# Four graph layers over 400000 sorted edges: 1400 chunks of edges counted densely where it was 1350, the last 50 with six rows of nodes

## The chip, the cores and the metric

The kernel runs on one core of one Trainium2 chip. The metric is the device time of one execution in microseconds, the median of three runs. One execution was profiled. The trace names the engines PE (TensorE; PEld are its weight loads), DVE (VectorE), ACT (ScalarE), POOL (GpSimd) and SP (SyncE).

## The reference

There are N = 12500 nodes with F = 64 features and E = 400000 edges, sorted by destination; sources are uniform, destinations lie as `12500 * u**2`, so low nodes have many edges and high ones few.

```python
x = _layernorm(x + _L0(edge_index, edge_type, x, ...))      # by source, with the relation: sigmoid(score) * x[dst], summed
x = _layernorm(x + _L1(x, src, dst, W, b))                  # h = segment_sum(x[src], dst), or x where there is no edge; h @ W.T + b
x = _layernorm(x + _L2(x, edge_index, edge_weight))         # segment_sum(x[src] * w, dst)
x = _layernorm(x + _L3(x, edge_index, edge_weight, edge_weight_n2))   # segment_sum(x[src] * (w2 * w), dst)
```

The first line sums over the source of each edge, the other three over its destination. These three are called the gather layers here, l = 0, 1 and 2 in the code; the first of them has no weights.

## The kernel before, in words

The edges are cut into C = 3125 chunks of 128, five chunks to a group (GC = 5). A gather layer sums a chunk in one of two ways.

**Dense**, for the first CD = 1350 chunks, whose destinations are so close that a chunk spans at most 3 to 5 nodes. For each chunk ScalarE makes the one-hot code of the source modulo 128 (`codes`, L921 to L932, times the weight in l = 1 and 2), and VectorE a one-hot tile of (source / 128, row) with rows x 98 columns by comparing a row of numbers with the chunk's key (`block_hots`, L1634). TensorE multiplies the two (`block_sums`, L1106); one to five chunks of a group form a block and are summed in one PSUM bank. VectorE adds each block into a window of 94 nodes (WC) in SBUF at a register offset (`block_add`, L1648). `PARTS` lists the ranges of chunks with the blocks in a group and the rows: (0, 200, (5,), 4) down to (1050, 1350, five blocks of one chunk, 5 rows), 1050 blocks in all. When a window is full (there are 28, two buffers), TensorE multiplies it with the features in 14 zones of seven matmuls (`flush_zone`, L1118), VectorE adds the result to the sums (`flush_add`, L1654), and ScalarE clears the zones (`clear`, L900).

**Tail**, for the remaining 1775 chunks, 355 steps of five (NT = 355). GpSimd gathers the 128 source rows of each chunk by an indirect DMA (L779) into a ring of R = 6 step buffers; VectorE makes the one-hot tile of the destinations (`tail_hots`, L1612) and in l = 1 and 2 weights it (`tail_weights`, L1621); TensorE sums the five chunks (L1139), and VectorE adds them (`tail_add`, L1663). Before the first gather of step n, GpSimd waits for TensorE's tail sum of step n - 6.

The order of both is written by a planner, `trailing_slots` (L121): it gives every block and every zone a cost, divides the sum by the number of steps less six, and puts blocks and zones into the steps of the tail as they come due (`BLOCK_END`, `ZONE_END`). In each step n TensorE does the block sums and zones that are due, then the tail sum of n. VectorE does the tail add of n - 1, the one-hot tiles of n + 2, the flush adds that are due, and for each block its add, followed by the tiles of later blocks for which there is room.

Room is given by rings. One-hot tiles and codes have BR = 10 chunks: a tile is made when the sum of the block ten chunks earlier is done. Block sums have PSD = 4 banks of PSUM (banks 0, 1, 2 and 6): the sum of block b waits for the add of block b - 4. Two banks (3, 4) hold tail sums, bank 5 the flush, bank 7 the row of numbers (`iota_p`, 490 columns).

Ahead of the layers stands the counting stage for the first line of the reference. It scatters the tail chunks from C0 = 1100 on with 2025 indirect DMAs of GpSimd (L700), 405 steps, with dense blocks of the first 1100 chunks beside them. Step by step SP loads rows of x: for groups of five-row chunks five small loads, for the later groups one of 64 rows. The keys of the dense chunks (`dense_keys`) are prepared here by VectorE.

## Time and profile before

| | us |
|---|---|
| median of 3 runs | 12297.09 |
| lowest, highest | 12291.68, 12302.24 |
| the profiled execution | 12289.04 |
| its span, first to last instruction | 12287.3 |
| mean granted TensorE clock | 0.775 of full |
| PE busy | 8780.1 (71%), 51577 instructions |
| DVE busy | 7811.6 (64%), 18656 |
| ACT busy | 5489.2 (45%), 12443 |
| POOL busy | 8308.1 (68%), 7419 |
| DMA | 410.51 MB, queue of POOL 16.1% and of SP 4.2% of 16 engines |

The busy shares are means over stages: about 3930 us of counting, some 160 us that finish the first line, and three gather layers of 2625 to 2691 us with normalisations between them. An fp32 matmul stands in the trace as two records. Waits that the page puts down to "remote" have a release that it can't name.

### The profile page before, as it was taken

What the parts mean: (1) busy time and instruction counts of PE and PEld (TensorE: products, weight loads), DVE (VectorE), ACT (ScalarE), POOL (GpSimd) and SP (SyncE); (2) the same over time, 40 slices, a digit from 0 to 9 for tenths busy, and PEclk for the clock granted to TensorE, in tenths of its full rate; (3) what the DMA queues carried; (4) which work ended last, traced back from release to release, by engine and by line L of the source; (5) the groups of instructions that cost most, each with busy time, mean ns of one, the idle gap of its engine ahead of it and who ended that gap; (6) DMA issues with size and microseconds to landing.
All of it is one profiled execution on the core that took longest, in us unless ns stands there. A gap on an engine that the chain in (4) does not pass through costs nothing. (4 is left out here: it accounts for less than half of the span.)

```text
span 12287.3 us, 173107 instructions
## 1 busy us (share of the span) xinstructions
PE 8780.1 (71%) x51577; PEld 6089.0 (50%) x51578; DVE 7811.6 (64%) x18656; ACT 5489.2 (45%) x12443; POOL 8308.1 (68%) x7419
## 2 busy tenths in 40 slices
PE   4777777777775455556656787777787787777776
PEld 2555556565554334444445445444445445444444
DVE  8777776766664765555554776656555776665655
ACT  4655544444442443333222665444433655444333
POOL 5888788888888566666665566666665566666665
PEclk7776777677776566676777898888888898888887
DMA  5333333333334211111111111111111111111111
GB/s 142 44 41 37 37 37 39 38 39 38 39 38 65 57 24 24 24 24 24 24 23 25 28 25 25 25 25 25 24 23 27 28 24 25 25 25 25 24 23 29
DMA packets 673100, 410.51 MB, mean 33 GB/s; under 512 B 473202, under 2 KB 582516, under 8 KB 670913
## 3 DMA queue, kind: packets, MB, share of 16 engines
q0 software_dynamic: 465120, 260.68, 16.1%
q1 hardware_dynamic: 203244, 135.37, 4.2%
q8 instruction: 432, 7.08, 0.2%
q10 hardware_dynamic: 3814, 3.37, 0.1%
q14 instruction: 490, 4.01, 0.1%
HBM read 291.44 MB, written 107.44 MB: 32 GB/s over the span
## 5 line engine op out<-in xcount | busy, mean ns | idle before, releaser
L779 POOL DMA_INDIRECT mem<-xt,mem x5325 | 5038.0, 946 | 3010.2 <-issue 1397.3
L1106 PE MATMUL ps<-mem 128*128 128x392 f32 (+5 forms) x6750 | 3015.5, 556 | 1108.3 <-issue 426.1
L700 POOL DMA_INDIRECT table<-mem,idx x2025 | 3154.4, 1558 | 749.6 <-issue 596.4
L1648 DVE TENSOR_TENSOR mem<-mem,ps 128x392 f32 (+2 forms) x3150 | 1802.8, 572 | 2143.1 <-remote 1243.3
L921 ACT ACTIVATE mem<-iota_f,mem 128x128 f32<-128x128 f32 x4050 | 1272.1, 390 | 2657.8 <-remote 1307.0
L1634 DVE TENSOR_SCALAR mem<-ps,mem 128x392 f32<-128x392 f32 (+5 forms) x4050 | 2456.5, 626 | 0.0
L1118 PE MATMUL ps<-mem,xs 128*64 128x94 f32 (+1 forms) x16464 | 2036.2, 279 | 473.9 <-issue 457.6
L1118 PEld LDWEIGHTS ps<-mem,xs 128*64 128x64 f32 (+1 forms) x16464 | 1758.5, 161 | 1129.8 <-issue 1091.2
L1106 PEld LDWEIGHTS ps<-mem 128*128 128x128 f32 (+1 forms) x6750 | 1156.1, 192 | 2019.8 <-issue 1452.7
L900 ACT COPY mem<-zero_c 128x658 f32<-128x658 f32 x1176 | 836.0, 732 | 1791.6 <-remote 1364.0
L1139 PE MATMUL ps<-mem 128*64 128x64 f32 (+1 forms) x10650 | 1120.8, 248 | 697.4 <-issue 675.9
L1139 PEld LDWEIGHTS ps<-mem 128*64 128x64 f32 (+1 forms) x10650 | 936.8, 159 | 1121.9 <-issue 1097.2
L984 PE MATMUL ps<-mem 128*128 128x392 bf16 (+2 forms) x2200 | 730.6, 471 | 585.5 <-DVE mem L1409 485.5
L1007 PE MATMUL ps<-mem 128*128 128x128 f32 x5684 | 866.4, 308 | 290.8 <-ACT mem L826 276.4
L1007 PEld LDWEIGHTS ps<-mem 128*128 128x128 f32 x5684 | 797.6, 219 | 344.6 <-ACT mem L826 320.1
L1424 DVE TENSOR_TENSOR acc<-acc,ps 128x512 f32<-128x512 f32 (+1 forms) x700 | 472.8, 677 | 745.2 <-PE ps L1007 660.5
L1663 DVE TENSOR_TENSOR acc<-acc,ps 64x64 f32 (+1 forms) x1065 | 223.0, 209 | 1044.9 <-remote 772.8
L1409 DVE TENSOR_TENSOR mem<-mem,ps 128x784 f32 (+2 forms) x800 | 787.8, 985 | 153.1 <-issue 67.0
L932 ACT ACTIVATE mem<-mem 128x128 f32<-128x128 f32 x2700 | 848.4, 390 | 17.7
L1035 PE MATMUL ps<-mem 64*128 64x64 f32 (+1 forms) x4050 | 719.5, 338 | 74.6 <-ACT mem L839 74.6
L1035 PEld LDWEIGHTS ps<-mem 64*128 64x128 f32 (+1 forms) x4050 | 655.2, 246 | 210.5 <-issue 102.4
L854 ACT COPY mem<-ps 128x320 f32<-128x320 f32 x405 | 171.8, 424 | 1250.5 <-DMA table<-mem,idx 832.2
(173 smaller groups left out, 7516.3 us busy)
## 6 DMA issues: line engine op xcount, KB each, us to landing
mem<-xt,mem POOLq DMA_INDIRECT x5325
mem<-key_rows SPq DMA_DIRECT2D x405, 160.0 KB
table<-mem,idx POOLq DMA_INDIRECT x2025
table<-mem POOLq DMA_DIRECT2D x3, 6304.0 KB
mem<-table SPq DMA_DIRECT2D x42, 448.0 KB, 5.2
xt<-xs SPq DMA_DIRECT2D x9, 896.0 KB
mem<-in_x_dram SPq DMA_DIRECT2D x413, 16.0 KB
mem<-in_x_dram SPq DMA_DIRECT2D x250, 1.2 KB
```

The costliest lines, as they stand in the source:

```text
L700: pool.indirect_dma_start(out=tables[i % NTAB][:, :], out_offset=bass.IndirectOffsetOnAxis(ap=idx[:, i % (IDXS * GC):i % (IDXS * GC) + 1], ...
L779: pool.indirect_dma_start(out=gbuf[:, o:o + F], out_offset=None, in_=xt[l][:, :], in_offset=bass.IndirectOffsetOnAxis(ap=src_q[q % 2].bitc ...
L900: act.copy(dense[zi // FZ % 2][:, lo * WC:hi * WC], zero_c[:, :].to_broadcast([P, (hi - lo) * WC])).then_inc(cleared[l], 1)
L921: ins = act.activation(lo_d[:, k * P:(k + 1) * P], iota_f[:, 0:P], ACT.Abs, bias=nslo_q[q % 2][:, c + k:c + k + 1])
L932: ins = act.mul(lo_l[:, o + k * P:o + (k + 1) * P], lo_d[:, k * P:(k + 1) * P], wd_q[q % 2][:, c + k:c + k + 1])
L1007: last = pe.matmul(ps_s[u % 2][:, k * P:(k + 1) * P], at_sb[u % 2][:, k * P:(k + 1) * P], xb[s_ % 2], start=True, stop=True)
L1035: last = pe.matmul(ps_m[:, k * F:(k + 1) * F], bts[0:kw, k * P:(k + 1) * P], rhs, start=True, stop=True)
L1106: last = pe.matmul(ps_d[b % PSD][:, 0:w], lo_l[:, r * P:(r + 1) * P], blk_l[:, r * DT:r * DT + w], start=(k == 0), stop=(k == parts - 1))
L1118: last = pe.matmul(ps_f[0:M, :], xs[:, t * XW:t * XW + M], dense[s_ % 2][:, t * WC:(t + 1) * WC], start=(t == 0), stop=(t == T - 1), skip_ ...
L1139: last = pe.matmul(ps_w[n % 2][0:M, :], gbuf[:, o:o + M], ohr[:, q:q + WD], start=(k == 0), stop=(k == GC - 1), skip_group_check=True)
L1634: ins = v.tensor_scalar(blk_l[:, r * DT:r * DT + w], iota_p[:, 0:w], kd_q[q % 2][:, at + k:at + k + 1], None, ALU.is_equal)
L1648: v.tensor_tensor(at, at, new, ALU.add).then_inc(d_add[l], 1)
```

## The change

CD goes from 1350 to 1400, so a layer has 345 steps of the tail and 1100 blocks. Chunks 1350 to 1399 are a new part with six rows each (D = 6), and since 6 x 98 = 588 columns are more than a bank of 512, each of these blocks is made in two halves of 294 columns: two one-hot comparisons, the second against a copy of the key less 294 (`kd_half`), two matmuls with the same weights into the two banks of a pair (`ps_d2`, banks 0 and 1 or 2 and 3), and one add over both banks. So that the four banks pair up, the tail sums move to banks 4 and 5 and the flush to bank 6. The new blocks take turns with two pairs: the sum of b waits for the add of b - 2, and the first of them for all adds before it. Their tiles use a ring of BX = 8 (`hot_after`). Windows stay 94 wide, but the largest offset in one is 88 and not 89; that gives 30 windows and not 28. With more blocks, more windows and fewer steps, the planner's cost of a step goes from 5.93 to 6.49. In the counting stage groups 270 to 279 now count as dense ones for SP's loads and for the keys.

```diff
-CD = 1350
+C6 = 1350
+CD = 1400
-D = 5
-DT = D * T
+D = 6
+DT = 5 * T
+DX = D * T
+BX = 8
-         (700, 1050, (1, 1, 1, 1, 1), 4), (1050, CD, (1, 1, 1, 1, 1), D)]
+         (700, 1050, (1, 1, 1, 1, 1), 4), (1050, C6, (1, 1, 1, 1, 1), 5),
+         (C6, CD, (1, 1, 1, 1, 1), D)]
+def hot_after(b):
+
+    c = BLOCKS[b][0] + BLOCKS[b][1] - 1
+    if c >= C6:
+        return BLOCK_OF[max(c - BX, C6 - 1)]
+    return BLOCK_OF[c - BR] if c >= BR else -1
-SEGS0, SEG_OF0 = segments(NB0, WD, 6)
+SEGS0, SEG_OF0 = segments(NB0, WD, 5)
-            if not is_block and z % FZ == 0 and zones[-1] < z:
+            if not is_block and z % FZ == 0 and (zones[-1] < z or blocks[-1] < SEGS[z // FZ + 1]):
+        kd_half = sb("kd_half", [P, CD - C6])
-        ps_d = [ps[:, k * BK:k * BK + DT] for k in (0, 1, 2, 6)]
-        ps_w = [ps[:, (3 + p) * BK:(3 + p) * BK + WD] for p in range(2)]
-        ps_f = ps[:, 5 * BK:5 * BK + WC]
+        ps_d = [ps[:, k * BK:k * BK + DT] for k in range(PSD)]
+        ps_d2 = [ps[:, 2 * p * BK:2 * (p + 1) * BK].rearrange("p (h c) -> p h c", h=2)[:, :, 0:DX // 2] for p in range(2)]
+        ps_w = [ps[:, (4 + p) * BK:(4 + p) * BK + WD] for p in range(2)]
+        ps_f = ps[:, 6 * BK:6 * BK + WC]
...
                     pe.wait_ge(blk_done[l], b + 1)
+                    if c >= C6:
+                        pe.wait_ge(d_add[l], b if c == C6 else b - 1)
+                        for h in range(2):
+                            at = (c - C6) % BX * DX + h * DX // 2
+                            last = pe.matmul(ps_d2[b % 2][:, h, :], lo_l[:, c % BR * P:(c % BR + 1) * P],
+                                             blk_l[:, at:at + DX // 2], start=True, stop=True)
+                        last.then_inc(blk_sum[l], 1)
+                        return
...
+                    link(v.tensor_scalar(kd_half[:, :], kd[:, C6:CD], -float(DX // 2), None, ALU.add))
...
                 def block_hots(b, l=l, blk_l=blk_l):
                     c, parts = BLOCKS[b]
-                    if c + parts > BR:
-                        v.wait_ge(blk_sum[l], BLOCK_OF[c + parts - 1 - BR] + 1)
+                    if hot_after(b) >= 0:
+                        v.wait_ge(blk_sum[l], hot_after(b) + 1)
...
+                    if c >= C6:
+                        r = (c - C6) % BX * DX
+                        v.tensor_scalar(blk_l[:, r:r + DX // 2], iota_p[:, 0:DX // 2], kd_q[q % 2][:, at:at + 1], None,
+                                        ALU.is_equal)
+                        v.tensor_scalar(blk_l[:, r + DX // 2:r + DX], iota_p[:, 0:DX // 2], kd_half[:, c - C6:c - C6 + 1],
+                                        None, ALU.is_equal).then_inc(blk_done[l], 1)
+                        return
...
-                    new = ps_d[b % PSD][:, 0:rows * T].rearrange("p (s d) -> p s d", s=T)
+                    if rows == D:
+                        at = dense_h[s_ % 2][:, :, :, at]
+                        new = ps_d2[b % 2].rearrange("p h (s d) -> p h s d", d=rows)
+                    else:
+                        at = dense_s[s_ % 2][:, :, at]
+                        new = ps_d[b % PSD][:, 0:rows * T].rearrange("p (s d) -> p s d", s=T)
                     v.tensor_tensor(at, at, new, ALU.add).then_inc(d_add[l], 1)
```

## Rows read from the trace of the kernel before

**Rows 1.** Busy time by stage: PE, PEld, DVE, ACT, POOL, granted clock, DMA, GB/s

```profile
1500.00:2500.00 1000.00, 759.28 (x4647) 587.07 (x4647) 697.57 (x2087) 494.15 (x934) 827.65 (x534) 0.73 0.38 38
4088.00:6713.00 2625.00, 1526.82 (x10369) 1177.54 (x10370) 1473.80 (x3136) 884.26 (x2000) 1673.63 (x1774) 0.69 0.11 24
6801.00:9487.00 2686.00, 2127.87 (x11718) 1304.88 (x11718) 1653.23 (x3488) 1302.84 (x3344) 1680.32 (x1774) 0.86 0.11 24
9541.00:12232.00 2691.00, 2116.90 (x11718) 1298.23 (x11718) 1654.71 (x3489) 1303.83 (x3345) 1680.91 (x1774) 0.87 0.11 24
```

**Rows 2.** Groups of instructions: count, busy us, mean ns, idle before and its releasers

```profile
L779 POOL DMA_INDIRECT mem<-xt,mem x5325 | 5038.0, 946 | 3010.2 <-issue 1397.3 <-remote 1026.7 <-PE ps L1139 542.5
L700 POOL DMA_INDIRECT table<-mem,idx x2025 | 3154.4, 1558 | 749.6 <-issue 596.4 <-ACT mem L854 123.5 <-DMA table<-mem,idx 27.3
L1612 DVE TENSOR_TENSOR mem<-ps,mem 128x320 f32<-128x320 f32 x1065 | 508.5, 478 | 0.8 <-issue 0.7
L1663 DVE TENSOR_TENSOR acc<-acc,ps 64x64 f32 (+1 forms) x1065 | 223.0, 209 | 1044.9 <-remote 772.8 <-PE ps L1139 208.8 <-issue 62.2
```

**Rows 3.** Gathers (L779) in 200 us: busy (count), clock; layers one and two

```profile
4088.00:4300.00 212.00, 139.06 (x148) 0.57 0.11 24
...
4700.00:4900.00 200.00, 126.34 (x135) 0.67 0.11 25
6850.00:7050.00 200.00, 111.94 (x118) 0.92 0.10 21
7450.00:7650.00 200.00, 124.64 (x132) 0.85 0.11 26
8850.00:9050.00 200.00, 127.75 (x135) 0.84 0.11 24
```

**Rows 4.** Block adds (L1648) in 200 us of layer two: 294 columns, then 490

```profile
7450.00:7650.00 200.00, 53.25 (x117) 0.85 0.11 26
8850.00:9050.00 200.00, 49.49 (x75) 0.84 0.11 24
```

**Rows 5.** One-hot tiles of dense chunks (L1634) in 200 us of layer two

```profile
6850.00:7050.00 200.00, 114.78 (x208) 0.92 0.10 21
7450.00:7650.00 200.00, 60.21 (x117) 0.85 0.11 26
8850.00:9050.00 200.00, 54.14 (x75) 0.84 0.11 24
```

**Rows 6.** Waits in layer two, 7000 to 9400 us: total, times, longest

```profile
POOL mem L779 <- remote: 314.4, 176, 2.7
POOL mem L779 <- PE ps L1139: 158.0, 74, 4.4
```

**Rows 7.** Order of time in layer two: start, us, instruction, idle before and releaser

```profile
7613.11 0.80 PE L1139 MATMUL ps<-mem 128*64 128x64 f32 x10
7617.70 0.94 POOL L779 DMA_INDIRECT mem<-xt,mem  x1 [0.30 <-issue]
7620.16 0.22 DVE L1663 TENSOR_TENSOR acc<-acc,ps 64x64 f32 x1 [1.95 <-remote]
7620.20 0.94 POOL L779 DMA_INDIRECT mem<-xt,mem  x1 [1.56 <-remote]
```

**Rows 8.** Tail adds (L1663) in two stretches at the end of layer two

```profile
9449.10:9467.10 18.00, 0.21 (x1) 0.72 0.09 19
9482.30:9491.80 9.50, 1.27 (x6) 0.55 0.08 17
```

**Rows 9.** Flush matmuls (L1118), 200 us of layer two: PE, PEld

```profile
8850.00:9050.00 200.00, 54.78 (x481) 46.87 (x481) 0.84 0.11 24
```

**Rows 10.** Block matmuls (L1106), 200 us: 294 columns, then 490

```profile
7450.00:7650.00 200.00, 92.39 (x236) 43.32 (x236) 0.85 0.11 26
8850.00:9050.00 200.00, 88.65 (x148) 27.14 (x147) 0.84 0.11 24
```

**Rows 11.** Order of time on POOL in the counting stage, the step with the keys

```profile
618.25 1.54 POOL L700 DMA_INDIRECT table<-mem,idx  x1 [5.51 <-DMA table<-mem,idx]
```

More of the change, by code:

```diff
@@ L335, in program @@
         rows1 = rows0 + 2 * ND0 + NTT
-        sbase, sbase0 = arena[0:1, rows1:rows1 + NSEG], arena[0:1, rows1 + 64:rows1 + 64 + NS0]
+        sbase, sbase0 = arena[0:1, rows1:rows1 + NSEG], arena[0:1, rows1 + 32:rows1 + 32 + NS0]
         nq_row = stat[0:1, 0:Q]
+        assert NSEG <= 32 and NS0 <= 32 and rows1 + 32 + NS0 <= 8455
         STAGED = AR + 2 * CQ * P + 2 * NTAB * BN
@@ L363, in program @@
         ps_s = [ps[:, (5 + p) * BK:(6 + p) * BK] for p in range(2)]
-        ps_d = [ps[:, k * BK:k * BK + DT] for k in (0, 1, 2, 6)]
-        ps_w = [ps[:, (3 + p) * BK:(3 + p) * BK + WD] for p in range(2)]
-        ps_f = ps[:, 5 * BK:5 * BK + WC]
-        ps_x = ps[:, 5 * BK + 2 * P:5 * BK + 3 * P]
+        ps_d = [ps[:, k * BK:k * BK + DT] for k in range(PSD)]
+        ps_d2 = [ps[:, 2 * p * BK:2 * (p + 1) * BK].rearrange("p (h c) -> p h c", h=2)[:, :, 0:DX // 2] for p in range(2)]
+        ps_w = [ps[:, (4 + p) * BK:(4 + p) * BK + WD] for p in range(2)]
+        ps_f = ps[:, 6 * BK:6 * BK + WC]
+        ps_x = ps[:, 6 * BK + 2 * P:6 * BK + 3 * P]
         iota_p = ps[:, 7 * BK:7 * BK + DT]
@@ L1552, in _ @@
             dense_s = [d.rearrange("p (s d) -> p s d", s=T) for d in dense]
+            dense_h = [d.rearrange("p (h s d) -> p h s d", h=2, s=T // 2) for d in dense]
             offs = Row(v, "dve_o", offs_i, WC - D)
@@ L1642, in block_add @@
                     rows = ROWS_OF[b]
-                    at = dense_s[s_ % 2][:, :, ds(offs.value(b), rows)]
+                    at = ds(offs.value(b), rows)
                     if b:
@@ L1665, in hots_up_to @@
                 def hots_up_to(b, added):
-                    while b < NBLK and (BLOCKS[b][0] + BLOCKS[b][1] <= BR or
-                                        BLOCK_OF[BLOCKS[b][0] + BLOCKS[b][1] - 1 - BR] < added):
+                    while b < NBLK and hot_after(b) < added:
                         block_hots(b)
```

## The prediction

> **What bounds the kernel now.** I read the busy time by stage first, then the pace of the gathers in stretches of 200 us, then the waits of GpSimd, and last the order of time around one step. The stages [rows 1]: the counting stage (a slice of it is shown) keeps GpSimd at 827.65 of 1000 us with 534 scatters, 1.87 us each, of which 1.558 us is the instruction itself [rows 2]; it is GpSimd's. Then come the three gather layers, 2625, 2686 and 2691 us, two thirds of the span. In none of them is an engine full: GpSimd is busy for 62 to 64%, VectorE for 56 to 62%, TensorE for 58% in the first and 79% in the others. What the reader should see is the next view: in the body of the layers 132 to 135 gathers are issued in 200 us [rows 3], one step of five gathers in 7.4 to 7.6 us. That holds in the first layer with bf16 blocks and in the second with fp32, at a granted clock of 0.67 and 0.84, and with 117 block adds in 200 us as with 75 [rows 4]. Only the opening of layers two and three is slower: 118 gathers in 200 us [rows 3], while VectorE makes 208 one-hot tiles there [rows 5], 0.96 us for a dense chunk.
>
> GpSimd alone could do a step in 5 x (0.946 + 0.30) = 6.2 us. It waits for TensorE's tail sums to free a gather buffer, 314.4 us in 176 waits whose event isn't shown plus 158.0 us in 74 that are put down to TensorE's line, in 2400 us of layer two [rows 6]. The order of time shows how [rows 7]: TensorE's tail sum is recorded at 7613.11, VectorE takes its result only at 7620.16, and GpSimd, which has issued the last gather of a step at 7617.70, goes on at 7620.20. So TensorE's results reach the other engines late and at about the time at which the last gather of a step has landed. By the Trainium skill (Perfetto Trace Analysis, Summary: the profiler window per engine type) the end of a TensorE instruction in a profile is an estimate, and the time until its semaphore is seen lies outside of it; that is the reading taken here, and no row tells which part of these 6 us it is. When there are no gathers left to issue, six tail adds come within 9.5 us, and while seven flush zones are due by the plan there is one add in 18 us [rows 8]. I read this as a pace of about 7.45 us that is tied to the cycle of the gathers as long as a step's dense work fits into it.
>
> **The change, part by part.** I sum against the profiled execution, 12289.04 us (span 12287.3 and 1.7 around it); the median of the runs is 8.05 us higher, and the sum is carried over to it.
>
> 1. Ten steps (of 355) go from each layer: 50 gathers of 0.946 us, 50 tail matmuls, ten tail adds of 0.209 us and ten one-hot tiles of 0.478 us [rows 2], with their weighting in two layers. At the mean pace of each layer, 2625/355 = 7.39, 7.57 and 7.58 us, that is 10 x 22.54 = **-225 us**. If the pace isn't the gathers', this term is only the work of the steps: on VectorE 0.69 us and the weighting, for which I estimate as much as for the tile: some -12 us a layer.
>
> 2. The planner puts the same early blocks into fewer steps: the first 30 steps of a layer hold 275 chunks and not 255 (worked out from the cost formula in the code). In layers two and three that opening goes by the chunk, 0.96 us each [rows 5]: 20 x 0.96 x 2 = **+38 us**. In layer one the opening is no slower than the body (148 gathers in its first 212 us [rows 3]), and I take nothing. The bound below is zero, the bound above 58 us (all three).
>
> 3. In the body the blocks come denser, 3.27 in a step and not 3.04. The trace has such a contrast: with 117 adds in 200 us there are 132 gathers, with 75 there are 135 [rows 3, 4]. That is 4.4 blocks in a step of 7.58 us against 2.8 in one of 7.41, 0.1 us for a block. 0.23 x 0.1 x 315 steps is 7 us a layer; with a step's work also made of more flush zones (1.33 and not 1.21) I take 12, **+36 us**. Below is zero; above, if each added flush zone is paid in full: 28 zones in a layer (two more windows of 14), each 1.59 us on TensorE (54.78 us for 481 records, 14 to a zone [rows 9]), 45 us a layer, 134 us in all.
>
> 4. The 50 new blocks of a layer. Each chunk is now two matmuls of 294 columns into two banks. A 294-column block takes 0.78 us on TensorE (92.39 us, 118 blocks), a 490-column one 1.20 us (88.65 us, 74 blocks) [rows 10], so two are 1.57 us: +0.37 over a block of five rows. VectorE makes two tiles of 294, 0.515 us each (60.21/117), where one of 490 takes 0.722 (54.14/75) [rows 5]: +0.31. Its add over 588 columns has no row; between 455 ns at 294 and 660 ns at 490 [rows 4] the slope is 1.05 ns a column, which gives an estimate of 0.76 us, +0.10. ScalarE's codes for 50 chunks lie beside it and are hidden by an engine that is idle more than half of the body. The new wait is on the sums: block b needs the add of b-2, where it was b-4, because two pairs of banks replace four. Behind this wait on TensorE are the flush zones and the tail sum of the step, and for the tail sum wait VectorE's next tail add and GpSimd's buffer. With 50 blocks in some 20 steps, 2.5 in each, this is where the pace may break. The bound below is zero; above, everything in series, 0.78 us for a block, 39 us a layer, and without limit by rows if the late arrival of [rows 7] is paid per pair. I take half of it, 20 us a layer, since the nearest rows (layer one's opening [rows 3], with blocks of five chunks and a ring with room for two) keep their pace: **+60 us**.
>
> 5. The switch from four banks to two pairs: the first new block waits for all adds, and the first eight new tiles for the last old sum. One drain of the chain, a block sum and an add and the way between, 3 to 7 us by [rows 7]; I take 5, **+15 us** for three.
>
> 6. The moved banks (tail sums, flush, fix-up) and the window of block offsets (88 and not 89 rows) cost nothing: the same instructions. On the destination indices of the inputs, cut into chunks of 128, no edge lies outside of its five or six rows or of its window, with the old bounds or the new, so the branches for stray edges stay empty.
>
> 7. The counting stage: groups 270 to 279 load ten times five small rows where it was one, on SP's queue; and the keys of the dense chunks are prepared in one run more, with the halved copy: eight linked VectorE instructions in one step. GpSimd's pace of 1.87 us covers the loads; in the step that holds this work GpSimd once waited 5.51 us [rows 11]. Eight more of these instructions at an estimated 0.5 us (a small one of this kind, the tile of 320 elements, takes 0.478 [rows 2]) are **+4 us** if paid in full, zero if not.
>
> Sum: -225 + 38 + 36 + 60 + 15 + 4 = **-72 us**: 12217 for the profiled execution, 12225 for the median.
>
> On TensorE's clock the rows show 0.69 granted in layer one, where the engine is busy for 58% of the time, and 0.86 and 0.87 in the others, at 79% [rows 1]: shares of the upper level, 2.4 GHz, in a mix with 1.2. The Trainium skill (TensorE: Matmul & The Clock Gate, What's actually happening) has it that activity releases the throttle; by that rule denser work would be paid back in part by the clock, and the trace agrees in direction. The sum by it would lose TensorE's share of item 4, 9 us a layer, and be near -99 us.
>
> **The rivals.** (a) The pace holds whatever is put into a step: only items 1, 2 and 7 count, -183 us, 12114. For it: 135 gathers with TensorE busy for 58% in one layer and 79% in the other. Against: the 132 at the densest stretch.
>
> (b) The two pairs of banks set the new stretch: if a pair of blocks needs one cycle of 7.4 us, 50 blocks take 186 us where 20 steps take 150; that is 36 us a layer more, in place of the 20 of item 4. With item 3 halfway to its upper bound (67 and not 36) it ends at 12225 + 48 + 31 = 12304: no change that can be told. For it: the adds follow the sums late. Against: room for two was enough in the opening of layer one.
>
> (c) Slower: TensorE, with the late arrival of its results, is the true bound, and the even pace is the planner's, which gives every step the same cost. Place: the body of all three layers. Price: the work added to it, 50 x 1.57 + 28 x 1.59 = 123 us a layer, less ten tail sums of about 1 us, 113 us a layer, 339 in all: 12636. It decides from the point at which a step's work no longer fits between two steps of gathers; if only half of it shows, 12467. For it: GpSimd waits in most steps, the steps at the end that hold only flush zones take as long as the others, 7 zones took 18 us [rows 8], and the planned cost of a step rises by 9% (5.93 to 6.49). Against: layer one, with 58% on TensorE, is only 2.3% shorter than layer two with 79%.
>
> (d) The change doesn't do what it says: a longer detour, like stray edges. By the indices there are none; 0.02. It would end above 12470.
>
> **How the numbers follow.** Forecast 0.48, (a) 0.12, (b) 0.15, (c) 0.23, (d) 0.02. The predicted time is the forecast's, 12225. The range takes in (a), (b) and the lower half of (c): 12105 to 12470, with about 0.04 below and 0.14 above. The forecast's own range is 12150 to 12270. A measurement tells about 0.2%, 25 us, from no change: faster 0.60 (the forecast and (a)), same 0.15, slower 0.25.
>
> **What would show it.** Right: 135 gathers in 200 us of the body as before, layers near 2590, 2665 and 2670 us, 1725 gathers in each. Item 2: the opening still at 0.96 us for a chunk. Item 4: in the last tenth of a layer, with adds of 588 columns at 0.76 us, gathers slow to no less than 125 in 200 us. Rival (b): under 115 there, with waits of TensorE's block sums for the block adds above the present ones. Rival (c): 125 or fewer gathers in 200 us in all of the body, and TensorE's busy share over 85% in layers two and three. I am wrong altogether if the counting stage moves by more than 15 us.

## The result and the profile after

The changed kernel takes 12106.87 us (median of 4 runs, 12100.94 to 12110.4), the kernel before beside it 12297.33: a ratio of 0.9847, interval 0.9835 to 0.9859. That is 190 us less where the forecast had 72, and within 8 us of rival (a), 12114. It lies 2 us above the lower end of the stated range, 12105, and outside of the forecast's own range of 12150 to 12270. The profiled execution has a span of 12108.7 us. Of all executions below one, of CD = 1450, took 12257.48 us at a granted clock of 0.586, where its three others took 10698 to 10705 us at 0.83 to 0.84; it is left out of the ratios.

Busy time by stage, for the stages of [rows 1] (PE, PEld, DVE, ACT, POOL, granted clock, DMA, GB/s):

```profile
1500.00:2500.00 1000.00, 758.58 (x4663) 586.23 (x4662) 696.21 (x2087) 495.99 (x938) 831.96 (x537) 0.73 0.38 38
4083.00:6649.00 2566.00, 1526.63 (x10769) 1193.09 (x10769) 1547.72 (x3268) 922.63 (x2088) 1626.69 (x1725) 0.71 0.11 24
6741.00:9369.00 2628.00, 2143.62 (x12210) 1321.20 (x12210) 1721.18 (x3611) 1358.49 (x3480) 1632.86 (x1724) 0.90 0.11 24
9425.00:12053.00 2628.00, 2132.14 (x12211) 1309.47 (x12212) 1721.93 (x3612) 1360.63 (x3480) 1632.54 (x1724) 0.91 0.11 24
```

The layers are shorter by 59, 58 and 62 us (first to last gather 2625.8, 2687.1 and 2691.5 us before; 2566.6, 2629.5 and 2629.2 after), each with ten steps fewer; they begin 5 us earlier. A mean step went from 7.40, 7.57 and 7.58 to 7.44, 7.62 and 7.62 us. TensorE and VectorE do more in less time, and the granted clock rose in every layer.

The pace is the old one all along. Gathers (now L796) in stretches of layers one and two, busy time of POOL with the count, clock, as in [rows 3]; then the block adds (L1687) in four of these stretches, as in [rows 4]:

```profile
4083.00:4295.00 212.00, 137.88 (x146) 0.60 0.11 24
4695.00:4895.00 200.00, 126.32 (x134) 0.69 0.11 24
6790.00:6990.00 200.00, 113.43 (x120) 0.96 0.10 22
7390.00:7590.00 200.00, 125.49 (x133) 0.89 0.11 25
8390.00:8590.00 200.00, 127.24 (x134) 0.86 0.11 25
9190.00:9340.00 150.00, 94.84 (x100) 0.93 0.10 23
```

```profile
4695.00:4895.00 200.00, 58.00 (x128) 0.69 0.11 24
7390.00:7590.00 200.00, 55.69 (x122) 0.89 0.11 25
8390.00:8590.00 200.00, 52.17 (x79) 0.86 0.11 25
9190.00:9340.00 150.00, 31.27 (x41) 0.93 0.10 23
```

The last stretch holds most of the 50 six-row blocks, and its 100 gathers in 150 us are 7.5 us a step: the pace of the rest. What the new blocks cost their engines is in the groups of equal shape (line, engine, operation, tiles, count, busy us, mean ns, idle before and its releasers):

```profile
L1122 PE MATMUL ps<-mem 128*128 128x294 f32 x400 | 135.9, 462 | 54.7 <-DVE mem L1687 43.3 <-issue 8.5 <-DVE mem L1663 1.6
L1687 DVE TENSOR_TENSOR mem<-mem,ps 128x588 f32 x150 | 114.1, 761 | 62.8 <-remote 34.1 <-PE ps L1122 15.1 <-issue 12.5
```

The add over 588 columns takes 761 ns, as estimated. TensorE's 400 records are the fp32 blocks of layers two and three; before them it was idle for 54.7 us, and 43.3 us of these are put down to VectorE's adds, the wait on b-2. The waits of layer two, 6940 to 9320 us (line waited for: us, times, longest), show that GpSimd waits about as it did in [rows 6]:

```profile
POOL mem L796 <- remote: 294.2, 173, 2.8
POOL mem L796 <- PE ps L1164: 198.1, 89, 5.7
PE ps L1131 <- DVE mem L1687: 100.9, 73, 5.7
PE ps L1122 <- DVE mem L1687: 20.8, 13, 6.6
```

So the gain is the ten steps, and almost nothing was paid for what they were exchanged for. The experiments ask three things: what sets the pace, what the dense work costs at it, and what the pace itself is made of.

### The profile page after: what moved, and what is told of

The parts are those of the page before. It is cut to its first block and busy times, and to the rows that moved or that the text cites. A ratio compares the mean times of both kernels' runs of the same rounds, so it can differ in the third digit from the quotient of the medians.

```text
span 12108.7 us, 177157 instructions
## 1 busy us (share of the span) xinstructions
PE 8810.7 (73%) x52953; PEld 6130.1 (51%) x52954; DVE 8021.3 (66%) x19055; ACT 5642.3 (47%) x12807; POOL 8169.7 (67%) x7269
## 3 DMA queue, kind: packets, MB, share of 16 engines
q8 instruction: 443, 7.26, 0.2%
## 5 line engine op out<-in xcount | busy, mean ns | idle before, releaser
L796 POOL DMA_INDIRECT mem<-xt,mem x5175 | 4895.3, 946 | 2973.9 <-issue 1331.8
L1131 PE MATMUL ps<-mem 128*128 128x392 f32 (+5 forms) x6750 | 2932.4, 540 | 1066.2 <-DVE mem L1687 425.9
L1687 DVE TENSOR_TENSOR mem<-mem,ps 128x392 f32 (+3 forms) x3300 | 1919.9, 582 | 1866.7 <-remote 990.2
L938 ACT ACTIVATE mem<-iota_f,mem 128x128 f32<-128x128 f32 x4200 | 1319.2, 390 | 2694.7 <-remote 1307.7
L1143 PEld LDWEIGHTS ps<-mem,xs 128*64 128x64 f32 (+1 forms) x17640 | 1807.7, 156 | 1033.7 <-issue 985.9
L917 ACT COPY mem<-zero_c 128x658 f32<-128x658 f32 x1260 | 896.5, 732 | 1430.1 <-remote 960.0
L1164 PE MATMUL ps<-mem 128*64 128x64 f32 (+1 forms) x10350 | 1043.4, 246 | 525.1 <-issue 505.4
L1164 PEld LDWEIGHTS ps<-mem 128*64 128x64 f32 (+1 forms) x10350 | 886.7, 158 | 949.7 <-issue 925.6
L1052 PE MATMUL ps<-mem 64*128 64x64 f32 (+2 forms) x4050 | 719.0, 338 | 74.7 <-ACT mem L856 64.6
L1052 PEld LDWEIGHTS ps<-mem 64*128 64x128 f32 (+2 forms) x4050 | 654.7, 245 | 210.9 <-issue 114.0
```

The source lines that it names most:

```text
L796: pool.indirect_dma_start(out=gbuf[:, o:o + F], out_offset=None, in_=xt[l][:, :], in_offset=bass.IndirectOffsetOnAxis(ap=src_q[q % 2].bitc ...
L917: act.copy(dense[zi // FZ % 2][:, lo * WC:hi * WC], zero_c[:, :].to_broadcast([P, (hi - lo) * WC])).then_inc(cleared[l], 1)
L938: ins = act.activation(lo_d[:, k * P:(k + 1) * P], iota_f[:, 0:P], ACT.Abs, bias=nslo_q[q % 2][:, c + k:c + k + 1])
L1052: last = pe.matmul(ps_m[:, k * F:(k + 1) * F], bts[0:kw, k * P:(k + 1) * P], rhs, start=True, stop=True)
L1131: last = pe.matmul(ps_d[b % PSD][:, 0:w], lo_l[:, r * P:(r + 1) * P], blk_l[:, r * DT:r * DT + w], start=(k == 0), stop=(k == parts - 1))
L1143: last = pe.matmul(ps_f[0:M, :], xs[:, t * XW:t * XW + M], dense[s_ % 2][:, t * WC:(t + 1) * WC], start=(t == 0), stop=(t == T - 1), skip_ ...
```

## The experiments

They were run in six groups, each beside the kernel before on the same chip. **There are two paces, by group**: the kernel before took 12289.99, 12202.6, 12292.42 and 12201.62 us in four groups (the slower pace, that of the result above), 10941.28 and 10942.37 in two. Times are compared within a group; where a time is held against one of another group, the text says so. The two groups at the faster pace ran on two chips, those at the slower one on three others, one of them met twice (12289.99 and 12202.6 us). That it is the chip that decides is likely by this and not shown. Of a code edit the first or the main lines are printed. Kernels that leave work out, and those with the smaller ring or with fewer waits on the changed kernel, were executed once. A "step" below is the time from the first to the last gather of a layer over its number of steps, for layers one, two and three.

### What sets the pace

**One gather of five in a step** (the tail sum uses its rows five times):

```diff
-                    for k in range(GC):
+                    for k in range(1):
                         o = (n % R) * GW + k * XW
```

> The changed kernel with one gather in a step where it has five; the four others are left out, and all five tail matmuls read the chunk that is there. All work of the other engines stays. Theory G (the cycle of a step's five gathers sets the pace of 7.4 to 7.6 us): the step falls to what the other engines need, about 4.5 us in layer one and 6 to 6.5 in the others, which takes 350 us or more off each layer; below 11100 us. Theory W (TensorE's dense work sets the pace, and the even pace is the planner's): 12107 us within 60. Theory V (VectorE's chain of adds and tiles sets it): the same as W.

9952.7 us beside 12289.99; steps of 4.81, 5.80 and 5.79 us. Stage 7000 to 9000 us of it, columns as above:

```profile
7000.00:9000.00 2000.00, 1872.39 (x11976) 1186.88 (x11975) 1707.62 (x3583) 1335.48 (x3427) 327.23 (x339) 0.98 0.05 11
```

With four of five gathers gone TensorE is busy for 94% at a clock of 0.98, and 5.8 us is what it needs for a step of the changed kernel in layers two and three; in layer one VectorE (busy for 92%) needs 4.8. Theory G is met: what the changed kernel takes beyond that, up to 7.44 and 7.62 us, belongs to the gathers. By itself this doesn't rule out rival (c), in which TensorE with its late results is the bound, since the late results may go with the gathers. The next run asks for that.

**The dense work made lighter**, with five gathers: one matmul of seven in each flush zone; block adds over one row only; a ring of four step buffers and not six.

```diff
-                    for t in range(*ZONES[z]):
+                    for t in (ZONES[z][0] if z < FZ - 1 else T - 1,):
```

> The changed kernel with one matmul in a flush zone where it has seven; the six others are left out, so TensorE loses six sevenths of 2079 us of flush matmuls, some 590 us a layer, 1.7 us of a step. Waits, adds and clears stay. Theory G: within 60 us of 12107. Theory W: the layers lose most of these 1.7 us a step, 400 to 590 us each; 10400 to 10900. Theory V: as G.

11918.91 us; steps of 7.26, 7.43 and 7.41. With some 1.7 us of TensorE's work gone from a step, and its busy share from 7000 to 9000 us down from 82 to 70%, the step loses 0.2 us of 7.6. The kernel ends about 180 us below the changed one, three times the 60 us of theory G and far from the 1200 to 1700 us of theory W: the dense work isn't quite free, and it isn't the bound, so rival (c) at its price is out. The granted clock fell with the work, from 0.90 to 0.82 in that stretch.

```diff
-                        at = dense_h[s_ % 2][:, :, :, at]
+                        at = dense_h[s_ % 2][:, :, :, at][:, :, :, 0:1]
```

> The changed kernel with block adds over one row of the block where it has three to six; the other rows are left out. VectorE's 3300 adds take about 0.2 us where they took 0.58, some 1.2 us a step. Theory G and theory W: within 60 us of 12107, if the later buffers come free a little earlier perhaps 50 us less. Theory V: 1.2 us off 1035 steps, about 10900.

12091.19 us, steps of 7.43, 7.57 and 7.62: VectorE's adds cost next to nothing, some 10 us of the kernel.

```diff
-R = 6
+R = 4
```

> The changed kernel with a ring of four step buffers for the gathers where it has six; the result is the same. In the kernel before, the tail add of a step comes 38 to 40 us after its gathers. If this lag is a fixed delay on the way (theory L), the step becomes 39/4 = 9.8 us and the kernel some 2000 us slower. If some engine has a fixed rate and the lag is only the queue ahead of it (G, W and V alike), the ring doesn't matter: within 60 us of 12107.

12083.25 us, steps of 7.43, 7.59 and 7.59. The tail add now trails the last gather of its step by 24 to 25 us and not by 39 to 40, so the ring is always full, whatever its size, and its size isn't what limits.

### What the parts of the change cost

**Six-row blocks alone**: chunks 1300 to 1349 get them, CD stays 1350, so 355 steps as before. At both paces:

```diff
-C6 = 1350
-CD = 1400
+C6 = 1300
+CD = 1350
```

> The changed kernel with C6 = 1300 and CD = 1350: 355 steps and 28 windows as before the change, but the last 50 dense chunks have six rows, two banks and a pair's turns. Its difference to the kernel before is the price of the blocks of six rows by themselves (items 4 and 5 of the prediction). Theory G (the gathers' cycle sets the pace, a step's dense work fits into it): 12297 us within 15. The prediction's items 4 and 5: some 0.41 us on VectorE and 0.37 on TensorE for each of 150 blocks in part, and three drains: 12297 + 75 = 12372.

> C6 = 1300 and CD = 1350 again, for the price of the six-row blocks at the other pace. With the kernel before at 12297 and steps of 7.4 to 7.6 us: theory G 12297 within 20; the prediction's items 4 and 5: 12372. With the kernel before at 10941: 10948 again, and nothing new.

At the faster pace 10947.59 us, a ratio of 1.0007 (0.9997 to 1.0016); at the slower one 12225.23 us, 1.0018 (1.0008 to 1.0028), beside 12202.6: 23 us (10 to 34) for items 4 and 5, where the prediction had 75 and theory G at most 20. The two profiles show what the paces are. Gathers of the stretch 7000 to 9000 us (busy POOL, count, clock), first at the faster, then at the slower pace, and GpSimd's waits at the faster one from 7000 to 8500 us:

```profile
7000.00:9000.00 2000.00, 1472.98 (x1553) 0.95 0.15 30
```

```profile
7000.00:9000.00 2000.00, 1273.70 (x1342) 0.87 0.13 25
```

```profile
POOL mem L796 <- issue: 364.8, 1197, 0.3
```

At the faster pace a step is 6.24 to 6.27 us, GpSimd's own 5 x (0.946 + 0.30), and it waits for nobody; the tail add trails the gathers by 3 us.

**The exchange rate**: the kernel before with 50 dense chunks fewer, the changed one with 50 and with 100 more (for these two the list of windows needs more room, so the source of zeros is half as wide).

```diff
-CD = 1350
+CD = 1300
```

> The kernel before with CD = 1300: 365 steps, 1000 blocks, 26 windows, planned cost of a step 5.44. Theory G: ten steps more in a layer at 7.4 to 7.55 us, 12297 + 3 x 74.5 = 12520, less 10 to 20 for a lighter opening. Theory W (dense work sets the pace): 50 blocks of five rows and 28 zones less, 1.2 and 1.59 us each, 105 us a layer: 12297 - 315 + 30 = 12010.

```diff
-CD = 1400
+CD = 1450
-zeros = arena[:, 8455:8455 + ROWS * F // P // 16]
+zeros = arena[:, 8849:8849 + ROWS * F // P // 32]
```

> The changed kernel with CD = 1450: 335 steps, 1150 blocks, 32 windows, planned cost of a step 7.08. (The source of the zeros for the tables is half as wide and read twice as often, so that the longer rows of indices have room; a few us at the start.) Theory G with the need of TensorE as the other bound, which the run with one gather puts at 5.8 us of a step: 5.8 x 7.08/6.49 = 6.3 us, still under 7.6, so another ten steps are saved: 12107 - 180 = 11927, within 40. Prediction's sum, with its give-backs: 12107 - 72 = 12035.

> The changed kernel with CD = 1500: 325 steps, 1200 blocks, 34 windows, planned cost of a step 7.71. TensorE's need by the same scaling is 5.8 x 7.71/6.49 = 6.9 us, near the 7.6 of the gathers' cycle. Theory G: 11927 - 170 = 11757, within 60; the pace in layers two and three would begin to give way, to 7.8 us. If the need of TensorE adds to the gathers' (theory A, each gather takes 0.45 us from TensorE, 7.6 = 5.8 + 4 x 0.45), a step is 6.9 + 1.8 = 8.7 us in layers two and three and the kernel is at 12250 or more, slower than with 1400.

All at the faster pace, against 10941.28 us: CD = 1300 11138.43, 1.0179 (1.0162 to 1.0196), that is +197 us for 30 steps more, 6.6 each (the expectation's two times were for the slower pace); CD = 1450 10703.94, 0.978 (0.9761 to 0.98); CD = 1500 10740.38, 0.9817 (0.9801 to 0.9833). Steps: 6.24, 6.27, 6.27; then 6.24, 6.43, 6.43; then 6.27, 6.77, 6.76. Here the mechanism of rival (c) sets in: from CD = 1450 on TensorE's need passes GpSimd's 6.24 us, and the ten steps less of 1500 lose more than they bring. The need could be forecast: 5.8 us scaled by the planned cost of a step gave 6.3 and 6.9 us, and layers two and three took 6.43 and 6.77. Stretch 7000 to 9000 us of CD = 1500:

```profile
7000.00:9000.00 2000.00, 1873.38 (x11751) 1187.15 (x11750) 1681.85 (x3401) 1287.99 (x3283) 1378.90 (x1440) 0.97 0.14 28
```

TensorE is at 94%, its level with a single gather in a step, and GpSimd issues 1440 gathers where it could 1600.

**The change and CD = 1450 at the slower pace**:

> The changed kernel itself. In the last group of runs the kernel before took 10941 us and not 12297, with a step of 6.24 us, which is GpSimd's five gathers and their gaps with nothing else, and without the stalls inside of TensorE's groups. If that is met again: theory G gives ten steps of 6.25 us in each of three layers, 10941 - 188 = 10755, within 15, since TensorE's 5.8 us fit into 6.24. With the other pace (kernel before at 12297): 12107 again.

> CD = 1450 again. With the kernel before at 12297: theory G (the larger of the gathers' cycle, 1.49 us for each of five, and TensorE's need of 6.3 us) 11930 within 40; theory A (each gather beyond the first takes 0.45 us from TensorE, on top of its need) 6.3 + 1.8 = 8.1 us in layers two and three, about 12250. With the kernel before at 10941: 10704 again.

The change: 12020.56 us, 0.9855 (0.9838 to 0.9871), the result once more. CD = 1450: 11875.14 us, 0.9736 (0.972 to 0.9752), steps of 7.41, 7.57 and 7.59. There is still room in a step at this pace: twenty steps less bring 327 us, ten bring 182. CD = 1450 beats the kernel before at either pace, and the changed one at the slower; at the faster pace the changed one wasn't run, and CD = 1500 wasn't at the slower.

### What the pace is made of

**Three gathers and four in a step** (as in the first experiment, with 3 and 4 for 1):

> The changed kernel with three gathers in a step where it has five; two are left out, and the tail matmuls of the last three chunks read the third. Theory G (a step is the larger of 1.49 us for each gather, 4.5 us, and the need of the other engines, which the run with one gather shows as 4.8 us in layer one and 5.8 in the others): about 9960 us, as with one gather. Theory A (each gather beyond the first takes 0.45 to 0.6 us from TensorE): 4.8 + 1.2 = 6.0 and 5.8 + 0.9 = 6.7 us, about 10900. If the kernel before is met at 10941, no stalls are there and theory A has nothing to act on: about 9960 by both.

> The changed kernel with four of the five gathers in each step (TensorE's fifth product takes the fourth chunk's rows; results are not the reference's). Theory C: a step takes 4 x 1.49 = 5.96 us in layer one and the larger of 5.96 and TensorE's 5.8 in the others, with few stalls of TensorE there: 10150 to 10250 in all. A rival F, in which the late answers set in only when the gathers are close to one another and cost a fixed 1.2 us a step over GpSimd's own 1.25 us a gather: 5.0 + 1.2 = 6.2 us in all layers, 10350 to 10450.

10050.8 us beside 12202.6 and 10803.25 us beside 12292.42. Theory A's 10900 for three gathers is out; theory G's 9960 is 91 us too low. Steps: 5.05, 5.82, 5.83 with three; 6.10, 6.40, 6.39 with four. In layer one, where the rest needs 4.8, that is GpSimd's 1.25 us for each gather and 1.3, 1.1 and 1.2 us on top (three, four, five gathers): a fixed part once in a step, rival F. By 1.49 us a gather three would have left layer one at its 4.8, and it took 5.05; of four gathers F had 6.2 and theory C 5.96, and 6.10 lies between them. In layers two and three it is 1.4, 0.2 more than F had. (The totals expected of four gathers were added up some 300 us too low; the steps are the test.) TensorE's groups of matmuls show stalls in their middle, where it waits for no semaphore. I count the pairs of neighbouring weight loads of one line that start over 0.6 us apart with no wait between them: 8 in layer two with one gather in a step, 14 with three, 104 with four, 350 with five (337 us from start to start; 287 pairs when the kernel was run again beside that with three gathers); none before the layers, and 22 at the faster pace. Some of these are no stalls, for at a granted clock of 0.50 a block's matmul alone comes near 0.6 us or over it. With the granted clock above 0.95 between the two loads the counts are 0, 3, 61 and 195 with one, three, four and five gathers, and 0 at the faster pace.

**Half the rows; a quarter of each row**, with as many gathers:

```diff
-                            out=gbuf[:, o:o + F], out_offset=None, in_=xt[l][:, :],
+                            out=gbuf[0:h, o:o + F], out_offset=None, in_=xt[l][:, :],
```

(h is 64 rows from the seventh step of the first layer on; the second kernel takes 16 numbers of a row in place of 64, and has no other edit.)

> The changed kernel with each gather taking 64 rows instead of 128 from the seventh step of the first layer on, so half the rows and half the bytes with as many gathers (the other half of each buffer keeps old data; results are not the reference's). Theory C, the cycle belongs to the count of gathers: a step stays at 7.4 to 7.6 us in all layers where the kernel before has 7.4 to 7.6, and the kernel within 60 us of the changed one. Rival L, the cycle is made by the landing of rows (descriptors or bytes): a step falls to GpSimd's own 6.2 us or to the 5.8 that TensorE needs, and the kernel to 10750 or less. If the kernel before runs at 6.24 us a step here, a fall below 6.24 shows only that GpSimd's instruction got shorter.

> The changed kernel with each gather taking rows of 16 numbers (64 bytes) instead of 64 (256 bytes) from the seventh step of the first layer on: as many gathers and rows, a quarter of the bytes, from the first quarter of the table (results are not the reference's). Theory C, count of gathers: a step stays at 7.4 to 7.6 us. Rival L in its form for bytes: 6.2 us or less, the kernel near 10750. Rival L in its form for descriptors: this one stays at 7.4 to 7.6 and the one with half the rows falls.

12104.79 and 12093.08 us beside 12292.42; steps of 7.44, 7.64, 7.60 and 7.43, 7.59, 7.60, and 331 and 322 stalls. Neither the rows nor the bytes that land matter: it is the number of gathers that counts, and rival L is out in both forms. GpSimd's groups in the two profiles:

```profile
L797 POOL DMA_INDIRECT mem<-xt,mem x5175 | 4689.3, 906 | 3178.4 <-issue 1318.2
```

```profile
L797 POOL DMA_INDIRECT mem<-xt,mem x5175 | 4892.4, 945 | 2957.4 <-issue 1325.2
```

With half the rows each instruction is 40 ns shorter, 0.2 us a step, and the step isn't: GpSimd waits longer instead. That the instruction took 945 ns with a quarter of the bytes, where it took 946, agrees with the Trainium skill (Perfetto Trace Analysis, DMA Instruction — SWDGE (GPSIMD)), by which its profiled end is when the descriptors have been written, not when the data have moved.

**Fewer waits**: GpSimd waits once for two or three free buffers and issues ten or fifteen gathers in a row.

```diff
-                    if n >= R:
-                        pool.wait_ge(agg_done[l], n - R + 1)
+                    if n >= R and n % 3 == 0:
+                        pool.wait_ge(agg_done[l], n - R + 3)
```

> The changed kernel in which GpSimd waits for a free buffer only before every second step of gathers, for two buffers at once (tail sum n - 4 and not n - 6), so ten gathers follow one another. Runs so far give a step as 1.25 us for each gather plus 1.1 to 1.4 us once a step (five gathers 7.44 and 7.62, four 6.10 and 6.39, three 5.05). Theory D: the fixed part is one pause of GpSimd for each wait, since TensorE's signals come through only while no gathers are being issued; with one wait for two steps a step takes 6.25 + 0.6 to 0.7 = 6.9 us, all layers together 2380 us each and less, the kernel near 11430. Rival E: TensorE is slowed by the gathers in flight themselves and GpSimd waits for it, as often as it is; the step stays at 7.4 to 7.6 and the kernel at 12050 to 12150, or comes out longer because the ring is in effect one step shorter.

> The same with one wait for three buffers before every third step (tail sum n - 3), fifteen gathers in a row. Theory D: 6.25 + 0.4 to 0.5 = 6.7 us a step, the kernel near 11200, if what a step holds for TensorE then still fits. Rival E: as before, 12050 to 12200; a stall of TensorE that grows with the run of gathers would make it longer still.

> CD = 1450 as before (335 steps; 7.41, 7.57 and 7.59 us a step at the slower pace, 6.24 and 6.43 at the faster one), and GpSimd waits once before every third step for three buffers, fifteen gathers in a row. The two runs with fewer waits fell on a group in which GpSimd never waits (6.24 us a step), so they could tell nothing of theory D. If the kernel before runs at 12200 to 12300 here: D (the fixed part is one pause for each wait) gives 6.25 + 0.4 to 0.5 us a step, 6.7, the kernel near 11000; E (TensorE is slowed by the gathers in flight) gives 7.4 to 7.6 as before, the kernel within 60 us of 11870, or longer. If the kernel before runs at 10940, both give 10700 and nothing is told apart.

The first two met the faster pace: 10828.65 and 10829.86 us beside 10942.37, with steps of 6.25, 6.36, 6.35 and 6.24, 6.37, 6.36. From 7000 to 8500 us GpSimd waits for nobody there, so they tell nothing of the pause. The third met the slower pace, and it takes **14125.84 us** beside 12201.62, 1.1581 (1.1562 to 1.16), with steps of 8.98, 10.18 and 10.15 us. Theory D had 11000. Without two of three waits it takes 2250 us more than the same kernel with all of them (11875 in another group, beside a kernel before of 12202.6). The wait before step n is also for a later tail sum, that of step n - 4 where it was n - 6, as with a smaller ring (the expectations say n - 3). No run parts this from the fifteen gathers in a row; a ring of four cost nothing above. The order of time shows what happens. One train of fifteen gathers in layer two, start us, us, engine, line, operation, tiles, count, idle before and releaser:

```profile
8505.01 0.94 POOL L796 DMA_INDIRECT mem<-xt,mem  x1 [11.26 <-PE ps L1164]
8507.21 0.58 DVE L1687 TENSOR_TENSOR mem<-mem,ps 128x392 f32 x1
8508.24 0.58 DVE L1687 TENSOR_TENSOR mem<-mem,ps 128x392 f32 x1
8509.26 0.58 DVE L1687 TENSOR_TENSOR mem<-mem,ps 128x392 f32 x1
...
8509.79 0.66 PEld L1164 LDWEIGHTS ps<-mem 128*64 128x64 f32 x10 [0.56 <-issue]
...
8516.51 0.56 DVE L1687 TENSOR_TENSOR mem<-mem,ps 128x392 f32 x1
8519.31 0.56 DVE L1687 TENSOR_TENSOR mem<-mem,ps 128x392 f32 x1 [1.71 <-PE ps L1131]
8521.60 1.14 PEld L1164 LDWEIGHTS ps<-mem 128*64 128x64 f32 x10 [1.10 <-issue]
8522.71 0.95 POOL L796 DMA_INDIRECT mem<-xt,mem  x1 [0.30 <-issue]
8523.54 0.56 DVE L1687 TENSOR_TENSOR mem<-mem,ps 128x392 f32 x1 [3.13 <-remote]
8524.25 1.65 PE L1131 MATMUL ps<-mem 128*128 128x392 f32 x2 [1.32 <-DVE mem L1687]
8526.38 0.56 DVE L1687 TENSOR_TENSOR mem<-mem,ps 128x392 f32 x1 [1.74 <-PE ps L1131]
8527.40 0.55 DVE L1687 TENSOR_TENSOR mem<-mem,ps 128x392 f32 x1
8528.40 0.58 DVE L1687 TENSOR_TENSOR mem<-mem,ps 128x392 f32 x1
...
8531.85 0.66 PEld L1164 LDWEIGHTS ps<-mem 128*64 128x64 f32 x10 [0.56 <-issue]
8532.92 0.95 POOL L796 DMA_INDIRECT mem<-xt,mem  x1 [9.26 <-PE ps L1164]
```

At the start of the train, at 8507, VectorE gets TensorE's block sums one each microsecond; in its second half one in three; from 8526.4 on, 1.6 us after the last data landed (8524.82 by the landings in the trace), again one each microsecond. The ten weight loads of a tail sum take 0.66 us early in the train as after it, and 1.14 us at 8521.60; that is the clock, which is granted at 0.50 from 8521.5 to 8522.8 and at 1.00 in the two other places. The busy times (PE, PEld, DVE, ACT, POOL, clock):

```profile
8505.00:8509.00 4.00, 3.50 (x11) 1.50 (x9) 3.96 (x11) 2.65 (x8) 3.08 (x4) 1.00 0.09 16
8513.00:8517.00 4.00, 1.69 (x4) 0.47 (x4) 2.86 (x8) 1.39 (x5) 3.09 (x4) 1.00 0.19 34
8517.00:8521.00 4.00, 1.88 (x4) 0.80 (x4) 1.70 (x4) 2.50 (x7) 3.08 (x4) 0.79 0.13 25
8526.00:8530.00 4.00, 4.00 (x19) 2.78 (x20) 3.62 (x8) 3.65 (x11) 0.00 (x0) 0.56 0.00 0
8530.00:8534.00 4.00, 4.00 (x35) 2.70 (x33) 2.33 (x6) 1.60 (x3) 0.95 (x1) 1.00 0.00 0
```

Over the 88 whole trains of 7600 to 10300 us (18.5 us each, then 11.7 us of pause) I counted TensorE's semaphore updates for sums of any kind, its weight loads and VectorE's block adds. The last column takes each block sum that ends in the stretch by the trace, and gives the median time until VectorE's add of it starts:

| time | updates per us | weight loads per us | block adds per us | us from sum to add |
|---|---|---|---|---|
| first 2 us of the train | 0.78 | 6.8 | 0.47 | 1.9 |
| 2 to 4 | 0.56 | 5.2 | 0.56 | 1.4 |
| 4 to 10 | 0.27 | 5.6 | 0.39 | 7.9 |
| 10 to 18 | 0.13 | 1.2 | 0.10 | 10.9 |
| first 2 us after its end | 0.14 | 0.7 | 0.11 | 5.1 |
| third us after it | 3.45 | 2.7 | 0.44 | 3.7 |
| fourth | 1.41 | 3.4 | 0.70 | 2.0 |
| 9 to 11.6 us after | 1.0 | 6.4 | 0.66 | 0.8 |

The updates are not all recorded, 1035 of 1150 for the block sums of the layer, and between 4 and 10 us the recorded ones of block sums (0.15 per us) are fewer than the adds that each need one (0.39). So the first column is too low there; the adds and their sums are complete, 1150 each, and the last column rests on them. From 4 us into a train on, the trace shows TensorE loading weights at its rate, while its sums are taken up 8 to 11 us after their recorded end. Then it has little left to start on, and a burst of updates comes 2 to 3 us after the train's end, 2.0 per us for block sums of which TensorE ends 0.1 per us at that time. As TensorE's recorded ends are modelled, no row tells whether the sums themselves are late or only their signals. The clock adds to the cost: it is granted at 0.72 from 10 us on and at 0.51 in the 4 us after the train, and over layer two at 0.80, where the kernel with all waits had 0.94.

So of theory D's premise the better part is shown (most signals come through where no gathers are in flight) and its conclusion is wrong: the rest of the step lives on these signals, and the longer train starves it. Rival E, TensorE's side slowed by gathers in flight and longer with their number in a row, is what was measured, with the later wait and the clock as parts that no run takes away.

## Why the prediction was right and wrong

**Direction, range, reading.** Faster, within 12105 to 12470. The reading of the first part held: the pace is tied to the cycle of the gathers as long as a step's dense work fits (one gather in a step: 5.8 us; three: 5.82; five: 7.62), and TensorE's results reach the others late while gathers are in flight, by 8 to 11 us in the trains of fifteen. The number is right in direction and in range by 2 us only, and the size is off: 190 us where the forecast had 72. The step that failed is the price of the added dense work, items 2 to 5: +149 us in the sum, 46 us measured (10, 13 and 23 us below). The sum didn't follow its own reading, by which dense work up to TensorE's need, 5.8 us in 7.6, was nearly free. I charged 38 us in item 2 by the pace of the opening, 36 in item 3 because one stretch had 132 gathers where others had 135, and 75 in items 4 and 5 of which 60 was half of an upper bound.

**Item 1**, -225 us: right. Ten steps at the mean pace are gone from each layer; the rest of the 190 is what all else cost. The mean step rose by 0.04, 0.05 and 0.04 us, times 345 steps some 46 us in all, where items 2 to 5 had 149 (worked out: 345 x 0.13 = 46). 225 - 46 and 5 us from an earlier start of the layers are 184; the profiled executions differ by 179, since the stretches between and after the layers are some 6 us longer, which no item had. The medians differ by 190, because the profiled execution of before was 8 us below its median and that of after 4 us above.

**Item 2**, +38: mis-sized. Layers two and three put 275 chunks into their first 30 steps as predicted, but these steps took 8.07 and 8.25 us where they took 8.18 and 8.23, so 0.88 us a chunk and not 0.96. The next 30 rose from 7.62 and 7.55 to 7.87 and 7.74. Both together are +4 and +6 us, 10 in all.

**Item 3**, +36: mis-sized; what the other items leave of the 46 is 13 us, a difference that takes item 4 from another group and is as unsure as its 10 to 34 us. The contrast of [rows 3, 4] was used beyond what it shows: with 122 adds in 200 us there are now 133 gathers, with 79 there are 134.

**Items 4 and 5**, +60 and +15: mis-sized, +23 measured at this pace (8 us a layer), +6 at the faster one, within its interval of nothing. The add was right (761 ns), the two matmuls of a chunk took 1.36 us (135.9 us for 100 chunks, at a granted clock of 0.93 in the layer's last stretch) where I had 1.57, and the wait was there, 13 times in layer two for 20.8 us. What failed is that these costs lie in series: the step hid most of them. The lower bound, zero, was the nearer end, by the even pace itself, and half of the upper bound had no row for it.

**Item 6**, nothing: no row shows a cost of it. **Item 7**, +4: the layers begin 5 us earlier, within the 15 allowed.

**Rivals.** (a), 12114 at a chance of 0.12, comes nearest, and that its time is within 8 us is in part luck: it charged 38 us for item 2, which measured 10, and nothing for items 3 to 5, which measured 36. (b) asked for under 115 gathers in 200 us at the end: there were 133. (c) asked for 125 or fewer and TensorE over 85%: there were 133 and 82%. Its evidence, GpSimd waiting in most steps, is explained by the late results while gathers are in flight, and two runs bear on its price: 1.7 us less work for TensorE in a step made it 0.2 us shorter, and CD = 1450 made it 0.04 to 0.06 us longer than the changed kernel beside it (7.35, 7.53 and 7.53). Its mechanism is real further on, at the faster pace from CD = 1450. (d): no.

**The clock.** It rose from 0.69, 0.86 and 0.87 to 0.71, 0.90 and 0.91 with the denser work, in the direction of the rule of the Trainium skill that the prediction cites (TensorE: Matmul & The Clock Gate, What's actually happening). The gain isn't due to it: steps did not get shorter.

**Still open**: by which path gathers in flight hold up TensorE's signals and its issue, whether it delays the sums or only their signals, and why only some groups show it. Gathers spaced out by a pause of GpSimd after every two or three, which the short trains suggest, were not tried, nor fifteen gathers in a row with a ring large enough to leave the wait at n - 6, nor the changed kernel itself at the faster pace.

## What to carry to other kernels

When the pace of a loop doesn't move between a stretch with light and one with heavy side work, take that as the rule for added side work, price it near zero up to the other engines' own need (here 46 us came of 149 charged), and put the doubt into the range. Find that need by one run that takes the pacing work away: scaled by the work, it tells how far such an exchange can go (at the faster pace to CD = 1450; 1500 was slower). And a wait that paces GpSimd's gathers can protect the others: with two of three removed and the third for a later sum the kernel took 19% more.

## What the runs showed of the hardware

- **With gathers in flight TensorE's results are taken up late**, in some groups of runs: in trains of 15 indirect DMAs, one every 1.25 us, VectorE's add started 1.9 us (median) after the recorded end of a block sum at the train's start, 7.9 us from 4 to 10 us on, 10.9 us from 10 to 18 us on, and 0.8 us well after the train; updates came in a burst of 3.45 per us 2 to 3 us after its end.
- **TensorE stalls within a group with it.** With the granted clock above 0.95, neighbouring weight loads started over 0.6 us apart, without a wait, 0, 3, 61 and 195 times in a layer with one, three, four and five gathers in a step, and never at the faster pace. The number of instructions counts: half the rows (331 by the count at any clock) and a quarter of the bytes (322) were near the 350 of the full gathers.
- **One core's program has two paces**: the same kernel took 10941 and 10942 us in two groups, 12202 to 12297 in five, with the same 0.946 us for a gather on GpSimd; the difference lies in the gather layers, 6.25 or 7.5 us a step.
- **A gather of 64 rows costs GpSimd 906 ns, of 128 rows 946**, at 256 bytes a row; 64 bytes a row, 945.
